# Decoder layer on one core: in the last group of heads VectorE turns the probabilities of tiles 0 and 1 and half of the values in 32x32 blocks

## The chip, the cores and the metric

The kernel runs on one core of a Trainium2 chip. The time is the device time of one execution in microseconds (us). The kernel before took 724.83 us, the median of 3 runs (724.61 to 726.72).

## The reference

A decoder layer on `x` of 8 sequences x 128 positions x 512 channels, in float32 (`_layernorm` has no weights):

```python
# 32 query heads, 8 key/value heads, head size 128; a group = 4 query heads and their key/value head
q, k, v = h @ w_q, h @ w_k, h @ w_v            # h = _layernorm(x)
scores  = einsum('bqhgd,bkhd->bhgqk', q, k) * 128 ** -0.5      # causal mask, softmax over keys
x = x + einsum('bhgqk,bkhd->bqhgd', probs, v).reshape(B, S, Hq * D) @ w_o
x = x + cross(ctx, ctx, _layernorm(x))         # softmax(ctx @ query^T), rows over query, then @ value
x = x + ffn(_layernorm(x))                     # silu(gate) * up, then down; weights unpacked from 4 bits
```

The output has the shape of `x`.

## The kernel before, in words

Every matmul of the attention is made in three passes: each operand is split into a rounded part (`_hi`) and the rest (`_lo`), and hi x hi, hi x lo and lo x hi are added in PSUM. ScalarE makes the hi parts by a copy; VectorE (out of PSUM) or GpSimd (out of SBUF) makes the lo parts by a subtraction.

There are 8 groups of heads (`LAST` is 7), and in each 8 tiles of 128 positions (tile b is sequence b). Groups 0 to 6 run as a loop with a deep pipeline of slots; the last group is written out by itself in `last_group`, one function for each engine, with 9 slots t = 0 to 8 and a short pipeline. Each engine takes its instructions strictly in the order in which its `last_group` issues them, and waits on semaphores. In a slot t:

- TensorE: `scores(t)`; the turning of the probabilities of tile t-1 through the array into PSUM bank `BK_T` (line 685, four 128x128 transposes); in slot 1 the turning of the second half of the values (`turn_values`, line 519); `fill` i, the projections of this group for the second half of the sequence range (12 matmuls each; 0 and 1 are keys and values, 2 to 5 queries) as `LAST_FILL` gives them; `values(t-1)` (probabilities x values, 3 matmuls); `out_heads(t-2)` (x `w_o`, 12 matmuls). From slot 3 on also `turn_queries(t-3)`, the first step of the cross attention of a tile. In slots 2 and 3 `out_heads` comes behind `values`, from slot 4 on (`EARLY`) ahead of it.
- VectorE: `mask(t)` (lines 1488 and 1492), `pt_lo` of tile t-1 (line 1543), `inverse(t)` (line 1498), `add_heads` (line 1424, which adds the output of `out_heads` to `xacc`), `heads_count` (lines 1288, 1289: mean and variance for the next layer norm), `heads_second(t-1)` (line 1503, `at_lo`).
- ScalarE: `pt_hi` of tile t-1 (line 996), `exponentials(t)` (line 919), the copies of the projections, `heads_first(t-1)` (line 951, `at_hi`), `second_norm(t-3)` (line 850, `xn`, the normalised tile that `turn_queries` turns), and in slots 0 and 1 the hi parts of the four `w_o` tiles (line 821).
- GpSimd: `normalise(t)` (line 1175), the lo parts of `w_o` (line 1160), and `inverse_deviation` (lines 1131 to 1136), which turns a variance into scale and shift for `xn`; in slot 2 for tile 0.

`out_heads(u)` of the last group always writes PSUM bank `BK_O`, so it waits until `add_heads(u-1)` has read it:

```python
pe.wait_ge(atlo_ready, step + u + 1 + PRIME)
pe.wait_ge(w_lo, g * UNITS + FIRST_UNITS + HG)
pe.wait_ge(o_added, step + u + PRIME - (g is not LAST))
```

In groups 0 to 6 the probabilities are turned by VectorE (`turn_probs`, line 1434: ten transposes of 32x32 blocks over four heads, the blocks above the diagonal being zero) from `probs` into the SBUF tile `pt`, and the values by sixteen such transposes (`turn_values`, line 1445) into `v_raw`; then GpSimd makes `pt_lo` and `v_lo`.

Of the kernel before, what the change touches and what calls it, by code (L numbers as in the profile page):

```python
# [7 lines left out]
ALU = mybir.AluOpType  # L8
# [14 lines left out]
PRIME = 2  # L23


def decoder_kernel(nc, x, ctx_in, ctx_turned, w_q, w_k, w_v, w_o,
# [26 lines left out]


    LAST_FILL = {0: [0, 1], 1: [2, 3], 2: [4], 3: [5]}
    LAST_TURN_V = 1
    LAST_SLOTS = NB + 1

    AT_NORM2, AT_SIM, AT_NORM3 = 3, 4, 6
# [21 lines left out]
    with ExitStack() as stack:  # L81
# [411 lines left out]
        def _(pe):  # L493
# [98 lines left out]
            def turn_queries(b):  # L592
                if 0 <= b < NB:
                    pe.wait_ge(ln_ready[1], b + 1)
                    if b >= 1:
                        pe.wait_ge(ln_hi[1], b)
                    else:
                        pe.wait_ge(vt_lo, NG * NH)
                    turn_tile(BK_XT, xn[:, b % 2, :]).then_inc(ln_turned[1], 1)

            def cross_output(b):
# [33 lines left out]
            def turn_values(g, n):  # L635

                pe.wait_ge(proj_out, g * NBLK + FIRST_BLOCKS + BLOCKS.index(("v", n)) + 1)
                pe.wait_ge(vt_lo, g * NH + (2 - n))
                turn_v(n)

            def fill(g, i):

                blocks = g * NBLK + FIRST_BLOCKS
                unit, n = BLOCKS[i]
                k = HBLK.index(unit)
                pe.wait_ge(w_lo, g * UNITS + (k + 1 if n == 1 else FIRST_UNITS + HG + k + 1))
                pe.wait_ge(proj_out, blocks + i - 1)
                project(unit, n, BK_PROJ[i % 2])
# [24 lines left out]
            def last_group():  # L673
                step = LAST * NB
                for t in range(LAST_SLOTS):
                    if t < NB:
                        scores(LAST, t)
                    if t >= 1:
                        u = t - 1
                        if u == 0:  # L680
                            pe.wait_ge(o_added, step + PRIME)
                        pe.wait_ge(prob_ready, step + u + 1)
                        pe.wait_ge(ptlo_ready, step + u + PRIME)
                        for j in range(HG):
                            mm = pe.transpose(psum[:, BK_T, j * P:(j + 1) * P], probs[:, u % 2, j, :], ident[:])
                        mm.then_inc(pt_done, 1)
                    if t == LAST_TURN_V:
                        turn_values(LAST, 1)
                    for i in LAST_FILL.get(t, ()):
                        fill(LAST, i)  # L690
                    cross_scores(t - AT_SIM)
                    if t >= EARLY:
                        out_heads(LAST, t - 2)
                    if t >= 1:
                        values(LAST, t - 1)
                    if 2 <= t < EARLY:
                        out_heads(LAST, t - 2)
                    turn_third(t - AT_NORM3)
                    turn_queries(t - AT_NORM2)
                    cross_output(t - AT_SIM)  # L700
# [117 lines left out]
        def _(act):  # L818
# [105 lines left out]
            def values_first(g, n):  # L924

                act.wait_ge(vt_done, 3 - n)
                act.wait_ge(pv_done, g * NB + (0 if n == 1 else BH) + PRIME)
                v_first(n)
# [60 lines left out]
            def last_group():  # L989
                step = LAST * NB  # L990
                for t in range(LAST_SLOTS):
                    if t >= 1:
                        u = t - 1
                        act.wait_ge(pt_done, u + 1 + PRIME)
                        act.wait_ge(pv_done, step + u + PRIME)
                        act.copy(pt_hi[:], psum[:, BK_T, :].rearrange("p (a b) -> p a b", a=HG)
                                 ).then_inc(pthi_ready, 1)
                    third_norm(t - AT_NORM3)
                    if t < NB:
                        exponentials(LAST, t)  # L1000
                    if t == LAST_TURN_V:
                        values_first(LAST, 1)
                    for i in LAST_FILL.get(t, ()):
                        fill_out(LAST, i)
                    if t >= EARLY:
                        cross_exp(t - AT_SIM)
                        second_norm(t - AT_NORM2)
                    if t >= 1:
                        heads_first(LAST, t - 1)
                    if t < EARLY:  # L1010
                        second_norm(t - AT_NORM2)
                    third(t - AT_NORM3)
                    queries_out(t - AT_NORM2)
                    for unit in SPLIT.get(t, ()):
                        if unit[0] == "o":
                            split_out(LAST, unit)
# [88 lines left out]
        def _(pool):  # L1105
# [66 lines left out]
            def normalise(g, t):  # L1172
# [3 lines left out]
                                   rowinv[:, t % 2, :].unsqueeze(2).to_broadcast([P, HG, P]),  # L1176
                                   ALU.mult).then_inc(prob_ready, 1)

            def group(g):
                n = 0  # L1180
                for t in range(SLOTS + 1):
                    if t in SPLIT_V:
                        half = slice(SPLIT_V[t] * BH, (SPLIT_V[t] + 1) * BH)
                        pool.wait_ge(vt_hi, g * NH + (3 - SPLIT_V[t]))
                        pool.tensor_tensor(v_lo[:, half, :], v_raw[:], v_hi[:, half, :].bitcast(F32),
                                           ALU.subtract).then_inc(vt_lo, 1)
                    if t < NB:
                        normalise(g, t)
                    if TURN <= t < NB + TURN:
                        pool.wait_ge(pthi_ready, g * NB + t - TURN + 1)  # L1190
                        pool.tensor_tensor(pt_lo[:], pt[:], pt_hi[:].bitcast(F32), ALU.subtract).then_inc(ptlo_ready, 1)  # L1191
                    for unit in SPLIT.get(t, ()):
                        n += 1
                        split_second(unit, g * UNITS + FIRST_UNITS + n)

            def last_group():
                n = 0
                for t in range(LAST_SLOTS):
                    if t < NB:
                        normalise(LAST, t)  # L1200
                    for unit in SPLIT.get(t, ()):
                        if unit[0] == "o":
                            n += 1
                            split_second(unit, LAST * UNITS + FIRST_UNITS + n)
                    cross(t)
# [69 lines left out]
        def _(dve):  # L1275
# [230 lines left out]
            def values_second(g, n):  # L1506

                dve.wait_ge(vt_hi, g * NH + (3 - n))
                v_second(n)
# [24 lines left out]
            def last_group():  # L1534
                step = LAST * NB
                for t in range(LAST_SLOTS):
                    if t < NB:
                        dve.wait_ge(pt_done, t - 1 + PRIME)
                        mask(LAST, t)
                    if t >= 1:  # L1540
                        u = t - 1
                        dve.wait_ge(pthi_ready, step + u + 1)
                        dve.tensor_tensor(pt_lo[:], psum[:, BK_T, :].rearrange("p (a b) -> p a b", a=HG),
                                          pt_hi[:].bitcast(F32), ALU.subtract).then_inc(ptlo_ready, 1)
                    cross_max(t - AT_SIM)
                    if 3 <= t < EARLY:
                        add_heads(LAST, t - 3)
                    if t < NB:
                        inverse(LAST, t)
                    cross_inverse(t - AT_SIM)  # L1550
                    if t > AT_SIM:
                        cross_add(t - AT_SIM - 1)
                        cross_count(t - AT_SIM - 1)
                    if t == EARLY - 1:
                        heads_count(LAST, t - 3)
                    if t >= EARLY:
                        add_heads(LAST, t - 2)
                        if t < NB:
                            heads_count(LAST, t - 2)
                    if t == LAST_TURN_V:  # L1560
                        values_second(LAST, 1)
                    if t >= 1:
                        heads_second(LAST, t - 1)
                    if t == EARLY:
                        scales()
                    if t == EARLY - 1:
                        add_heads(LAST, t - 2)
                        heads_count(LAST, t - 2)
                    if t == NB:
                        heads_count(LAST, t - 2)  # L1570
                    third_second(t - AT_NORM3)
# [152 lines left out]
```

## Time and profile before

| | us |
|---|---|
| median of 3 runs | 724.83 |
| the profiled execution | 724.8 |
| its span (first to last instruction) | 723.0 |
| TensorE busy | 705.2 (98%) |
| VectorE busy | 617.4 (85%) |
| ScalarE busy | 384.8 (53%) |
| GpSimd busy | 397.9 (55%) |
| the last group's slots 0 to 3 on TensorE | 501.5 to 532.3 |
| mean granted TensorE clock | 0.996 |

How to read it: the busy share of TensorE counts the time in which at least one matmul is in flight. In a timeline the difference between the starts of two matmuls is what one of them holds the engine; the duration shown is longer, since they overlap. A time in square brackets at the end of a timeline row is how long the engine sat idle before the instruction, and who released it.

### The profile page before, as it was taken

What the parts mean: (1) busy time and instruction counts of PE and PEld (TensorE: products, weight loads), DVE (VectorE), ACT (ScalarE), POOL (GpSimd) and SP (SyncE); (2) the same over time, 40 slices, a digit from 0 to 9 for tenths busy, and PEclk for the clock granted to TensorE, in tenths of its full rate; (3) what the DMA queues carried; (4) which work ended last, traced back from release to release, by engine and by line L of the source; (5) the groups of instructions that cost most, each with busy time, mean ns of one, the idle gap of its engine ahead of it and who ended that gap; (6) DMA issues with size and microseconds to landing.
All of it is one profiled execution on the core that took longest, in us unless ns stands there. A gap on an engine that the chain in (4) does not pass through costs nothing.

```text
span 723.0 us, 11410 instructions
## 1 busy us (share of the span) xinstructions
PE 705.2 (98%) x3450; PEld 586.2 (81%) x3450; DVE 617.4 (85%) x1387; ACT 384.8 (53%) x966; POOL 397.9 (55%) x376
## 2 busy tenths in 40 slices
PE   8999999999999999999999999999999889999995
PEld 8888888888888888888888888888877657888874
DVE  6589888988898898889888988988378888898897
ACT  4566535635562655365455636563556555655643
POOL 4375536545463655266445626561445535789886
PEclk9999999999999999999999999999999999999998
DMA  9523036105701550251046003402900002322103
GB/s 299 173 72 106 1 120 218 41 0 146 225 8 30 172 167 0 94 183 52 0 116 201 2 8 98 148 0 71 338 14 0 1 1 58 88 58 67 30 12 116
DMA packets 44902, 63.92 MB, mean 88 GB/s; under 512 B 4462, under 2 KB 23278, under 8 KB 44878
## 3 DMA queue, kind: packets, MB, share of 16 engines
q1 hardware_dynamic: 44878, 63.62, 28.3%
q8 instruction: 12, 0.20, 0.1%
q14 instruction: 12, 0.10, 0.1%
HBM read 52.67 MB, written 10.95 MB: 88 GB/s over the span
## 4 chain that ended last, share of the span: by engine, by line
PE 88%; DVE 5%; POOL 2%; ACT 2%; issue 2%; POOLq 0%; DVEq 0%; ACTq 0%
PE psum L500 21%; PE psum L499 21%; PE psum L501 21%; PE psum L630 8%; PE psum L716 5%; PE psum L717 5%; PE psum L739 2%; PE psum L738 2%; PE psum L526 1%; DVE stats L1288 1%; ACT probs L919 1%; PE psum L505 1%; POOL o_sum L1243 1%; DVE xprobs L1414 1%; DVE negmax L1492 0%
## 5 line engine op out<-in xcount | busy, mean ns | idle before, releaser
L1434 DVE STREAM_TRANSPOSE pt<-probs 32x128 f32<-32x128 f32 x560 | 168.9, 302 | 9.1 <-POOL pt_lo L1191 2.3
L1175 POOL TENSOR_TENSOR probs<-probs,rowinv 128x512 f32<-128x512 f32 x64 | 76.5, 1195 | 156.0 <-DVE rowinv L1498 156.0
L919 ACT ACTIVATE probs<-probs,negmax 128x128 f32<-128x128 f32 x256 | 99.9, 392 | 116.0 <-DVE negmax L1492 116.0
L499 PE MATMUL psum<-xt_hi,wq_hi 128*128 128x512 f32 x256 | 102.7, 401 | 0.0
L499 PE MATMUL psum<-wo_hi,at_hi 128*128 128x512 f32 x256 | 100.2, 392 | 0.5 <-DVE at_lo L1503 0.5
L501 PE MATMUL psum<-xt_hi,wq_lo 128*128 128x512 f32 x256 | 99.8, 390 | 0.0
L500 PE MATMUL psum<-xt_lo,wq_hi 128*128 128x512 f32 x256 | 99.8, 390 | 0.0
L501 PE MATMUL psum<-wo_hi,at_lo 128*128 128x512 f32 x256 | 99.6, 389 | 0.0
L500 PE MATMUL psum<-wo_lo,at_hi 128*128 128x512 f32 x256 | 99.6, 389 | 0.0
L1191 POOL TENSOR_TENSOR pt_lo<-pt,pt_hi 128x512 fp32r<-128x512 f32 x56 | 72.4, 1293 | 24.2 <-ACT pt_hi L982 24.1
L630 PEld LDWEIGHTS psum<-kt,qt 128*128 128x128 f32 x512 | 66.8, 191 | 6.5 <-issue 1.4
L716 PE MATMUL psum<-ft_hi,gw 128*128 128x512 f32 (+1 forms) x176 | 70.5, 400 | 1.2 <-DVE ft_lo L1297 0.9
L1445 DVE STREAM_TRANSPOSE v_raw<-vt 32x128 f32<-32x128 f32 x224 | 67.5, 301 | 3.5
L717 PE MATMUL psum<-ft_lo,gw 128*128 128x512 f32 (+1 forms) x176 | 69.0, 392 | 0.0
L630 PE MATMUL psum<-kt,qt 128*128 128x128 f32 x512 | 67.4, 274 | 0.3 <-ACT qt L833 0.3
L833 ACT ACTIVATE qt<-psum 128x512 f32<-128x512 f32 x64 | 37.7, 589 | 54.1 <-PE psum L501 54.0
L499 PEld LDWEIGHTS psum<-wo_hi,at_hi 128*128 128x128 f32 x256 | 48.1, 188 | 11.0 <-DVE at_lo L1503 1.2
L501 PEld LDWEIGHTS psum<-xt_hi,wq_lo 128*128 128x128 f32 x256 | 48.1, 188 | 10.1
L501 PEld LDWEIGHTS psum<-wo_hi,at_lo 128*128 128x128 f32 x256 | 48.0, 188 | 10.0
L1424 DVE TENSOR_TENSOR xacc<-psum,xacc 128x512 f32<-128x512 f32 x64 | 44.1, 688 | 14.2 <-PE psum L501 12.5
L500 PEld LDWEIGHTS psum<-wo_lo,at_hi 128*128 128x128 f32 x256 | 48.1, 188 | 9.8
L951 ACT CAST at_hi<-psum 128x512 fp32r<-128x512 f32 x64 | 37.1, 579 | 35.6 <-PE psum L501 34.3
(158 smaller groups left out, 1576.2 us busy)
## 6 DMA issues: line engine op xcount, KB each, us to landing
wq_raw<-in_L_attn_w_q SPq DMA_DIRECT2D x8, 1024.0 KB, 5.6
wo_raw<-in_L_attn_w_o SPq DMA_DIRECT2D x8, 1024.0 KB, 7.8
u_zn<-zeros_gu SPq DMA_DIRECT2D x16, 344.0 KB, 6.3
unpacked_w<-u_q SPq DMA_DIRECT2D x8, 688.0 KB, 7.8
gw<-unpacked_w SPq DMA_DIRECT2D x20, 256.0 KB, 3.5
unpacked_w<-u_q SPq DMA_DIRECT2D x6, 512.0 KB, 6.7
u_q<-in_L_ffn_gate_qweight SPq DMA_DIRECT2D x8, 344.0 KB, 5.7
u_q<-in_L_ffn_up_qweight SPq DMA_DIRECT2D x8, 344.0 KB, 4.1
```

Of the source, the lines that this page charges most:

```text
L499: pe.matmul(dst, a_hi, b_hi, start=start, stop=False)
L500: pe.matmul(dst, a_hi, b_lo, start=False, stop=False)
L501: return pe.matmul(dst, a_lo, b_hi, start=False, stop=stop)
L630: mm = pe.matmul(psum[:, BK_S, j * P:(j + 1) * P], qt[:, j, t * P:(t + 1) * P], kt[:, t * P:(t + 1) * P], start=True, stop=True)
L716: pe.matmul(dst, gw[:, r, m, c, 0:w], ft_hi[:, c, cols], start=True, stop=False)
L717: return pe.matmul(dst, gw[:, r, m, c, 0:w], ft_lo[:, c, cols], start=False, stop=True)
L919: e = act.activation(probs[:, t % 2, j, :], probs[:, t % 2, j, :], ACT.Exp, bias=negmax[:, t % 2, j:j + 1], accum_out=rowsum[:, t % 2, j:j ...
L1175: pool.tensor_tensor(probs[:, t % 2], probs[:, t % 2], rowinv[:, t % 2, :].unsqueeze(2).to_broadcast([P, HG, P]), ALU.mult).then_inc(prob_ ...
L1191: pool.tensor_tensor(pt_lo[:], pt[:], pt_hi[:].bitcast(F32), ALU.subtract).then_inc(ptlo_ready, 1)
L1424: dve.tensor_tensor(xacc[:, u, :], psum[:, out_bank(g, u), :], xacc[:, u, :], ALU.add).then_inc(o_added, 1)
L1434: turned = dve.transpose(pt[keys, :, queries], probs[queries, t % 2, :, keys])
L1445: turned = dve.transpose(v_raw[keys, :, heads], vt[heads, n, :].rearrange("p (a b) -> p a b", a=BH)[:, :, keys])
```

## The change

In the last group, tiles 0 and 1 (`LAST_BLOCKS` = 2) are now turned by VectorE with `turn_probs` into `pt`, in slots 0 and 1; their `pt_hi` is copied by ScalarE from `pt`, and their `pt_lo` made by GpSimd (`probs_second`). The second half of the values is turned by VectorE in slots 1 (6 blocks) and 2 (10 blocks); its hi part is copied by ScalarE in slot 3, its lo part made by GpSimd in slot 3, ahead of `normalise(3)`. Tiles 2 to 7 are turned by TensorE as before. On TensorE, the turning of tile 2 in slot 3 moves behind `fill` 5, and `out_heads` stands ahead of `values` in slots 2 and 3 too. `turn_queries(0)` waits for one `vt_lo` less.

```diff
--- before.py
+++ after.py
@@ -53,7 +53,9 @@
 
 
     LAST_FILL = {0: [0, 1], 1: [2, 3], 2: [4], 3: [5]}
-    LAST_TURN_V = 1
+    LAST_BLOCKS = 2
+    LAST_TURN_V = {1: (0, 6), 2: (6, 16)}
+    LAST_SPLIT_V = 3
     LAST_SLOTS = NB + 1
 
     AT_NORM2, AT_SIM, AT_NORM3 = 3, 4, 6
@@ -595,7 +597,7 @@
                     if b >= 1:
                         pe.wait_ge(ln_hi[1], b)
                     else:
-                        pe.wait_ge(vt_lo, NG * NH)
+                        pe.wait_ge(vt_lo, NG * NH - 1)
                     turn_tile(BK_XT, xn[:, b % 2, :]).then_inc(ln_turned[1], 1)
 
             def cross_output(b):
@@ -675,25 +677,27 @@
                 for t in range(LAST_SLOTS):
                     if t < NB:
                         scores(LAST, t)
-                    if t >= 1:
+                    if t == LAST_BLOCKS + 1:
+                        for i in LAST_FILL[t]:
+                            fill(LAST, i)
+                    if t > LAST_BLOCKS:
                         u = t - 1
-                        if u == 0:
+                        if u == LAST_BLOCKS:
                             pe.wait_ge(o_added, step + PRIME)
                         pe.wait_ge(prob_ready, step + u + 1)
                         pe.wait_ge(ptlo_ready, step + u + PRIME)
                         for j in range(HG):
                             mm = pe.transpose(psum[:, BK_T, j * P:(j + 1) * P], probs[:, u % 2, j, :], ident[:])
                         mm.then_inc(pt_done, 1)
-                    if t == LAST_TURN_V:
-                        turn_values(LAST, 1)
-                    for i in LAST_FILL.get(t, ()):
-                        fill(LAST, i)
+                    if t != LAST_BLOCKS + 1:
+                        for i in LAST_FILL.get(t, ()):
+                            fill(LAST, i)
                     cross_scores(t - AT_SIM)
-                    if t >= EARLY:
+                    if t >= EARLY or 2 <= t <= LAST_BLOCKS + 1:
                         out_heads(LAST, t - 2)
                     if t >= 1:
                         values(LAST, t - 1)
-                    if 2 <= t < EARLY:
+                    if LAST_BLOCKS + 1 < t < EARLY:
                         out_heads(LAST, t - 2)
                     turn_third(t - AT_NORM3)
                     turn_queries(t - AT_NORM2)
@@ -991,15 +995,18 @@
                 for t in range(LAST_SLOTS):
                     if t >= 1:
                         u = t - 1
-                        act.wait_ge(pt_done, u + 1 + PRIME)
+                        if u < LAST_BLOCKS:
+                            act.wait_ge(pt_turned, step + u + 1)
+                        else:
+                            act.wait_ge(pt_done, u - LAST_BLOCKS + 1 + PRIME)
                         act.wait_ge(pv_done, step + u + PRIME)
-                        act.copy(pt_hi[:], psum[:, BK_T, :].rearrange("p (a b) -> p a b", a=HG)
-                                 ).then_inc(pthi_ready, 1)
+                        act.copy(pt_hi[:], pt[:] if u < LAST_BLOCKS else
+                                 psum[:, BK_T, :].rearrange("p (a b) -> p a b", a=HG)).then_inc(pthi_ready, 1)
+                    if t == LAST_SPLIT_V:
+                        values_rounded(LAST, 1)
                     third_norm(t - AT_NORM3)
                     if t < NB:
                         exponentials(LAST, t)
-                    if t == LAST_TURN_V:
-                        values_first(LAST, 1)
                     for i in LAST_FILL.get(t, ()):
                         fill_out(LAST, i)
                     if t >= EARLY:
@@ -1176,19 +1183,27 @@
                                    rowinv[:, t % 2, :].unsqueeze(2).to_broadcast([P, HG, P]),
                                    ALU.mult).then_inc(prob_ready, 1)
 
+            def values_second(g, n):
+
+                half = slice(n * BH, (n + 1) * BH)
+                pool.wait_ge(vt_hi, g * NH + (3 - n))
+                pool.tensor_tensor(v_lo[:, half, :], v_raw[:], v_hi[:, half, :].bitcast(F32),
+                                   ALU.subtract).then_inc(vt_lo, 1)
+
+            def probs_second(g, u):
+
+                pool.wait_ge(pthi_ready, g * NB + u + 1)
+                pool.tensor_tensor(pt_lo[:], pt[:], pt_hi[:].bitcast(F32), ALU.subtract).then_inc(ptlo_ready, 1)
+
             def group(g):
                 n = 0
                 for t in range(SLOTS + 1):
                     if t in SPLIT_V:
-                        half = slice(SPLIT_V[t] * BH, (SPLIT_V[t] + 1) * BH)
-                        pool.wait_ge(vt_hi, g * NH + (3 - SPLIT_V[t]))
-                        pool.tensor_tensor(v_lo[:, half, :], v_raw[:], v_hi[:, half, :].bitcast(F32),
-                                           ALU.subtract).then_inc(vt_lo, 1)
+                        values_second(g, SPLIT_V[t])
                     if t < NB:
                         normalise(g, t)
                     if TURN <= t < NB + TURN:
-                        pool.wait_ge(pthi_ready, g * NB + t - TURN + 1)
-                        pool.tensor_tensor(pt_lo[:], pt[:], pt_hi[:].bitcast(F32), ALU.subtract).then_inc(ptlo_ready, 1)
+                        probs_second(g, t - TURN)
                     for unit in SPLIT.get(t, ()):
                         n += 1
                         split_second(unit, g * UNITS + FIRST_UNITS + n)
@@ -1196,6 +1211,10 @@
             def last_group():
                 n = 0
                 for t in range(LAST_SLOTS):
+                    if 1 <= t <= LAST_BLOCKS:
+                        probs_second(LAST, t - 1)
+                    if t == LAST_SPLIT_V:
+                        values_second(LAST, 1)
                     if t < NB:
                         normalise(LAST, t)
                     for unit in SPLIT.get(t, ()):
@@ -1535,9 +1554,14 @@
                 step = LAST * NB
                 for t in range(LAST_SLOTS):
                     if t < NB:
-                        dve.wait_ge(pt_done, t - 1 + PRIME)
+                        if 2 <= t < LAST_BLOCKS + 2:
+                            dve.wait_ge(pt_turned, step + t - 1)
+                        elif t >= LAST_BLOCKS + 2:
+                            dve.wait_ge(pt_done, t - 1 - LAST_BLOCKS + PRIME)
                         mask(LAST, t)
-                    if t >= 1:
+                    if t in LAST_TURN_V:
+                        turn_values(LAST, 1, *LAST_TURN_V[t])
+                    if t > LAST_BLOCKS:
                         u = t - 1
                         dve.wait_ge(pthi_ready, step + u + 1)
                         dve.tensor_tensor(pt_lo[:], psum[:, BK_T, :].rearrange("p (a b) -> p a b", a=HG),
@@ -1557,8 +1581,8 @@
                         add_heads(LAST, t - 2)
                         if t < NB:
                             heads_count(LAST, t - 2)
-                    if t == LAST_TURN_V:
-                        values_second(LAST, 1)
+                    if t < LAST_BLOCKS:
+                        turn_probs(LAST, t)
                     if t >= 1:
                         heads_second(LAST, t - 1)
                     if t == EARLY:
```

## Rows read from the trace of the kernel before

**Rows 1.** The page of the profile, busy time and the chain that ended last.

```profile
PE 705.2 (98%) x3450; PEld 586.2 (81%) x3450; DVE 617.4 (85%) x1387; ACT 384.8 (53%) x966; POOL 397.9 (55%) x376
...
PE 88%; DVE 5%; POOL 2%; ACT 2%; issue 2%; POOLq 0%; DVEq 0%; ACTq 0%
```

**Rows 2.** Timeline, TensorE, slots 1 to 4 (start us, duration us, engine, line, tiles).

```profile
508.69 0.60 PE L685 MATMUL psum<-ident,probs 128*128 128x128 f32 x4
509.13 0.60 PE L519 MATMUL psum<-ident,vt 128*128 128x128 f32 x4
509.49 0.48 PE L499 MATMUL psum<-xt_hi,wq_hi 128*128 128x512 f32 x1
...
515.02 0.39 PE L499 MATMUL psum<-pt_hi,v_hi 128*128 128x512 f32 x1
...
520.48 0.39 PE L499 MATMUL psum<-wo_hi,at_hi 128*128 128x512 f32 x1
...
523.21 1.05 PE L630 MATMUL psum<-kt,qt 128*128 128x128 f32 x8
524.09 0.60 PE L685 MATMUL psum<-ident,probs 128*128 128x128 f32 x4
524.45 0.48 PE L499 MATMUL psum<-xt_hi,wq_hi 128*128 128x512 f32 x1
...
527.30 0.39 PE L499 MATMUL psum<-pt_hi,v_hi 128*128 128x512 f32 x1
...
527.98 0.39 PE L499 MATMUL psum<-wo_hi,at_hi 128*128 128x512 f32 x1
...
531.76 0.66 PE L505 MATMUL psum<-ident,xn 128*128 128x128 f32 x4 [0.89 <-ACT xn L850]
```

**Rows 3.** Timeline, VectorE, the same slots.

```profile
505.75 0.18 DVE L1498 RECIPROCAL rowinv<-rowsum 128x4 f32<-128x4 f32 x1 [1.72 <-ACT probs L919]
...
509.69 0.69 DVE L1492 TENSOR_REDUCE negmax<-probs 128x4 f32<-128x512 f32 x1
...
525.69 0.68 DVE L1543 TENSOR_TENSOR pt_lo<-psum,pt_hi 128x512 fp32r<-128x512 f32 x1
526.29 0.68 DVE L1424 TENSOR_TENSOR xacc<-psum,xacc 128x512 f32<-128x512 f32 x1
527.50 0.18 DVE L1498 RECIPROCAL rowinv<-rowsum 128x4 f32<-128x4 f32 x1 [0.53 <-ACT probs L919]
```

**Rows 4.** Timeline, ScalarE, group 6 (first row) and the same slots.

```profile
466.12 0.62 ACT L982 CAST pt_hi<-pt 128x512 fp32r<-128x512 f32 x1 [0.45 <-DVE pt L1434]
...
504.06 0.40 ACT L919 ACTIVATE probs<-probs,negmax 128x128 f32<-128x128 f32 x1 [2.42 <-DVE negmax L1492]
...
524.73 0.59 ACT L996 CAST pt_hi<-psum 128x512 fp32r<-128x512 f32 x1 [3.46 <-PE psum L685]
...
530.89 0.81 ACT L850 ACTIVATE xn<-xacc,shift,rstd 128x512 f32<-128x512 f32 x1 [2.12 <-POOL shift L1136]
```

**Rows 5.** Timeline, GpSimd, the same slots.

```profile
506.01 1.04 POOL L1175 TENSOR_TENSOR probs<-probs,rowinv 128x512 f32<-128x512 f32 x1 [3.00 <-DVE rowinv L1498]
...
517.09 2.55 POOL L1160 TENSOR_TENSOR wo_lo<-wo_raw,wo_hi 128x512 fp32r<-128x512 f32 x2 [3.69 <-ACT wo_hi L821]
```

**Rows 6.** Timeline, VectorE, group 6, where it turns probabilities.

```profile
462.95 3.13 DVE L1434 STREAM_TRANSPOSE pt<-probs 32x128 f32<-32x128 f32 x10
```

**Rows 7.** Timeline, TensorE, its two longest idle times behind the start.

```profile
706.47 0.50 PE L738 MATMUL psum<-int_hi,dw 128*128 128x512 f32 x1 [1.09 <-DVE o_sum L1642]
...
713.94 1.86 PE L812 MATMUL psum<-ident,o 128*128 128x128 f16 x16 [1.26 <-POOL o L1262]
```

**Rows 8.** Windows near the end: PE, PEld, DVE, ACT, POOL busy; granted clock; DMA.

```profile
713.00:714.00 1.00, 0.06 (x1) 0.09 (x2) 1.00 (x3) 0.40 (x1) 1.00 (x2) 0.99 0.00 0
714.00:715.00 1.00, 1.00 (x11) 1.00 (x12) 1.00 (x3) 0.00 (x0) 1.00 (x2) 0.50 0.00 0
...
717.00:718.00 1.00, 0.91 (x12) 0.73 (x10) 0.98 (x2) 0.28 (x1) 0.78 (x1) 0.81 1.03 385
```

## Prediction, made before the changed kernel was run

> **What bounds the kernel now.** I read the page first: TensorE is busy for 98% of the span and carries 88% of the chain that ended last [rows 1]. So a change elsewhere costs or gives only what it does to TensorE's order of work. Then I read the timelines of the last group, since the diff touches nothing else, TensorE first. From 508.69 to 530.87 one matmul follows the other; the only idle time is the 0.89 us before `turn_queries(0)` at 531.76, which waits for `xn` [rows 2]. The timelines of the three other engines show what stands in front of that `xn` [rows 3 to 5]. From slot 4 on the diff changes no order, so the question is only how much later or earlier `turn_queries(0)` starts; what follows is built on it and on itself, and I take it to move as a block.
>
> **What TensorE is spared.** The turning of tile 0 held it 0.44 us (509.13 less 508.69), that of the values 0.36 (509.49 less 509.13), that of tile 1 as much as tile 2, 0.36 (524.45 less 524.09) [rows 2]. Sum 1.16 us. Moving the turning of tile 2 behind `fill` 5 and `out_heads` ahead of `values` removes no work.
>
> **What VectorE gains in work.** Ten blocks of probabilities take 3.13 us [rows 6], twice 6.26; the values' sixteen blocks at the same 0.313 each 5.0. It is spared three subtractions of 0.68 [rows 3], 2.0. Net 9.2 us more in slots 0 to 2, where it was mostly idle. I follow it in order of time, with the handovers of the rows.
>
> Slots 0 and 1. `inverse(0)` at 505.75, `normalise(0)` on GpSimd 506.01 to 507.05 [rows 3, 5]. Turn tile 0: 507.1 to 510.24. `mask(1)` can't start before, so its second instruction stands at 511.0 where it stood at 509.69 [rows 3]. Six blocks of the values: to 513.5. `exponentials(1)` starts 0.7 us after that second instruction, and the inverse 1.69 after the exponentials' start (505.75 less 504.06 [rows 3, 4]), 513.4: both are ready at 513.5. `normalise(1)` to 514.8; turn tile 1: 514.85 to 518.0. Then `at_lo(0)`, to 518.7. TensorE meanwhile has no transposes: `fill` 2 and 3 (5.53 us, 515.02 less 509.49) from 508.7 to 514.2, `values(0)` 0.68 to 514.9, `scores(2)` 0.88, `fill` 4 2.85, to 518.6 [rows 2]. GpSimd makes `pt_lo(0)` from 511.7 to 513.0, in time.
>
> Slot 2. `out_heads(0)` was at 520.48 behind `values(1)` [rows 2]; now it stands directly behind `fill` 4 and wants `at_lo(0)` (518.7) and the last `w_o` lo part. That one starts with ScalarE's copies, which follow `at_hi(0)`, 0.8 us earlier than before: GpSimd 516.3 where it was 517.09, plus 2.55, 518.85 [rows 5]. TensorE waits about 0.3 us; `out_heads(0)` 518.9 to 521.7 (2.73, 523.21 less 520.48, and 0.1 for the first matmul after a wait), `values(1)` to 522.3, `scores(3)` to 523.2, `fill` 5 to 526.05. On VectorE `mask(2)`, then ten blocks of values, 519.9 to 523.1, `inverse(2)`, `at_lo(1)` to 523.9, `mask(3)` to 525.2. `prob_ready(2)` is there at 524.4, ahead of the turning. All this is covered by `fill` 5.
>
> Slot 3. The turning of tile 2 starts at 526.05 and ends at 526.4, where it ended at 524.45 [rows 2]. Now cover is missing. `pt_hi(2)` starts 0.25 later, T = 526.65 (it was 524.73, 0.28 after the turning [rows 4]). VectorE sits at `pt_lo(2)` until T + 0.62, and queued behind it is `add_heads(0)`, T + 1.22 to T + 1.9 (0.60 from start to start, 0.68 long [rows 3]). `out_heads(1)` uses the same bank and waits for that add. Before, `fill` 5 and `values(2)` stood between the turning and `out_heads(1)`: 527.98 less 524.45, 3.53 us of cover, and the add was over by 526.97 [rows 2, 3]. Now nothing stands between them. TensorE idles from 526.4 to T + 1.95 = 528.6: **2.2 us**. Then `out_heads(1)` 2.84 to 531.4, `values(2)` to 532.1.
>
> `turn_queries(0)`. Two chains lead to `xn(0)`. One: `exponentials(3)` on ScalarE is queued behind `pt_hi(2)` and the new copy of `v_hi` (0.52 each from start to start), so it starts at T + 1.05 = 527.7, `inverse(3)` at 529.4, where it was 527.50; from there to `xn(0)` it was 3.39 us (530.89 less 527.50 [rows 3, 4]), so 532.8. Two: ScalarE's `at_hi(2)` is queued ahead of `xn(0)` and wants `values(2)`: 532.1 + 0.2 + 0.5 = 532.8. Both end at once. TensorE turns at 532.8 + 0.87 = 533.65 (531.76 less 530.89) and has idled 1.5 us instead of 0.89. So **+1.9 us** at this point. Check by the account: 0.3 + 2.2 + 1.5 idle less 0.89, less 1.16 spared, is 1.95. GpSimd's new `v_lo` (1.3) stands ahead of `normalise(3)`; it ends at 535.0 and TensorE wants it at 535.05 behind `scores(4)`: free, by a hair.
>
> GpSimd's subtraction out of SBUF, 1.3 us where VectorE took 0.68, and ScalarE's copy out of `pt`, 0.62 where it took 0.59 out of PSUM [rows 4], are in these times. No transfer is touched.
>
> **The clock.** An idle time of 1.26 us near the end, before line 812, was followed by the clock's fall from 2.4 to 1.2 GHz (0.99 granted in 713 to 714, 0.50 in 714 to 715); it was back at full speed within 717 to 718, whose mean of 0.81 puts the return at 717.4. The idle of 1.09 us before 706.47 was not followed by a fall [rows 7, 8]. The change makes an idle time of 2.2 us with transposes ahead of it, and one of 1.5. Longer than the one that led to a fall: I take it that the clock falls once here. A stretch of 3.4 us at half speed, full of matmuls of `out_heads(1)` and `values(2)`, costs at most 1.7 us; part of it may lie in the idle time, so 1.6. The second chain to `xn(0)` passes it on whole.
>
> The Trainium skill (TensorE: Matmul & The Clock Gate, section Why this matters for your kernels) warns only of idle gaps longer than this change makes; by that rule the clock stays and the time is that of the first rival. The trace has a fall after 1.26 us, which speaks against leaning on it.
>
> The Trainium skill (VectorE: DVE Perf Modes, section Rules for kernel authors) says that a 128x128 transpose belongs on TensorE where PSUM will do as its destination. The rows agree on the price, 0.36 us of TensorE against 3.13 of VectorE for a tile of four heads [rows 2, 6]; had VectorE no idle time the change would cost some 9 us. It has it in slots 0 to 2.
>
> **The sum.** The profiled execution took 724.8 us (span 723.0), which is the median too: 724.8 + 1.9 + 1.6 = **728.3 us**.
>
> **Rivals.**
> - *The clock stays at 2.4 GHz.* For it: idle times of 0.89 and 1.09 us left it alone, and dense matmuls stand around these. Against: 1.26 led to a fall. Then 724.8 + 1.9 = 726.7, which is not slower by what can be told. If the fall comes in some executions alone, the median is one of the two.
> - *The waits are covered after all* (`add_heads(0)` is over in time, `xn(0)` no later in relation to the work). Then only the spared 1.16 us is left, 723.6. The code speaks against it: bank, order and wait are fixed. Even with the 0.89 us gone too it would be 722.7, so hardly faster by 0.3%.
> - *Turning the tiles by VectorE takes longer and more is late*: if the blocks of tile 1 and its `at_lo(0)` came 1 us later (GpSimd's order, blocks slowed by it), `out_heads(0)` and all behind it would move by the same; with the fall 729.3.
> - *The chain's length is over-told*: both chains and the 2.2 us shrink by some tenths each, and some later wait absorbs a part. Then 725.5 to 726.5.
>
> **Chances.** A measurement here can tell about 0.3%, 2.2 us: faster is below 722.65, slower above 727.0. Fall of the clock 0.50 (nearly all slower); clock stays 0.32 (a quarter of it above 727.0); more is late 0.06; chain over-told 0.09; covered 0.03. So slower 0.64, same 0.34, faster 0.02. Range: from 725.9, which leaves out 0.1 at the bottom, to 729.2, which takes in a late `out_heads(0)` beside the fall.
>
> **What would show it.** Right: TensorE idle about 2.2 us before the first matmul of `out_heads(1)` (line 499, `wo_hi`), released by VectorE's add to `xacc`; idle about 1.5 us before the first turning of `xn`; ten blocks of 3.13 us twice; the granted clock at 0.50 for some us from about 529. Wrong: the granted clock at 1.00 there (then 726.7); `out_heads(1)` without idle; a shift at `scores(5)` other than at `turn_queries(0)`; or idle before `out_heads(0)` of much over 0.3 us.

## The result and the profile after

The changed kernel took 728.34 us, the median of 6 runs (727.94 to 728.76), against 724.83 us of before, the median of 6 (724.59 to 726.72). The ratio is 1.004 (95% interval 1.0028 to 1.0051): slower by 3.5 us. The forecast was 728.3.

The page after, busy times and shares of the chain, which answer to [rows 1]:

```profile
PE 706.3 (97%) x3438; PEld 586.2 (81%) x3438; DVE 626.1 (86%) x1420; ACT 384.4 (53%) x966; POOL 401.1 (55%) x379
...
PE 87%; DVE 6%; POOL 3%; issue 2%; ACT 2%; POOLq 0%; DVEq 0%; ACTq 0%
```

TensorE has 12 matmuls fewer, VectorE 8.7 us more work, and the span went from 723.0 to 726.6. The busy shares tell nothing of where 3.6 us went. The timeline of TensorE in the last group does (it answers to [rows 2]; start, duration, engine, line, tiles, idle time before and who released it). The first row is `scores(0)`, where the last group starts:

```profile
501.55 1.05 PE L632 MATMUL psum<-kt,qt 128*128 128x128 f32 x8
...
518.96 0.47 PE L501 MATMUL psum<-wo_hi,at_hi 128*128 128x512 f32 x1 [0.24 <-DVE at_lo L1522]
...
526.11 0.60 PE L690 MATMUL psum<-ident,probs 128*128 128x128 f32 x4
...
528.79 0.47 PE L501 MATMUL psum<-wo_hi,at_hi 128*128 128x512 f32 x1 [2.09 <-DVE xacc L1443]
...
532.94 0.63 PE L501 MATMUL psum<-pt_hi,v_hi 128*128 128x512 f32 x1
...
535.46 0.66 PE L507 MATMUL psum<-ident,xn 128*128 128x128 f32 x4 [1.39 <-ACT xn L854]
```

Three idle times stand in it. The second, 2.09 us before `out_heads(1)`, is new and is ended by line 1443, the add into `xacc`. `out_heads(1)` then takes 4.15 us (532.94 less 528.79) where twelve matmuls took 2.73 [rows 2].

VectorE in slot 3 (it answers to [rows 3]):

```profile
527.36 0.69 DVE L1567 TENSOR_TENSOR pt_lo<-psum,pt_hi 128x512 fp32r<-128x512 f32 x1 [2.06 <-ACT pt_hi L1003]
527.97 0.68 DVE L1443 TENSOR_TENSOR xacc<-psum,xacc 128x512 f32<-128x512 f32 x1
529.42 0.18 DVE L1517 RECIPROCAL rowinv<-rowsum 128x4 f32<-128x4 f32 x1 [0.78 <-ACT probs L923]
```

It sat idle for 2.06 us at `pt_lo(2)` with `add_heads(0)` queued behind it, although `out_heads(0)` had been issued in full by 521.8 (518.96 plus 2.84), 6.2 us before the add started. ScalarE's rows answer to [rows 4]:

```profile
526.74 0.58 ACT L1003 CAST pt_hi<-psum 128x512 fp32r<-128x512 f32 x1 [3.48 <-PE psum L690]
527.22 0.62 ACT L938 CAST v_hi<-v_raw 128x512 fp32r<-128x512 f32 x1
...
534.11 0.58 ACT L955 CAST at_hi<-psum 128x512 fp32r<-128x512 f32 x1 [4.23 <-PE psum L503]
534.59 0.82 ACT L854 ACTIVATE xn<-xacc,shift,rstd 128x512 f32<-128x512 f32 x1
```

`xn` stands behind `at_hi(2)`, which waits for `values(2)`: the second chain of the prediction. And the granted clock (window; PE, PEld, DVE, ACT, POOL busy; granted share of the clock; DMA share, GB/s):

```profile
529.00:530.00 1.00, 1.00 (x5) 0.81 (x5) 0.58 (x2) 0.87 (x4) 0.00 (x0) 1.00 0.00 0
530.00:531.00 1.00, 1.00 (x4) 0.78 (x3) 0.36 (x2) 0.00 (x0) 0.38 (x2) 0.55 0.00 0
...
533.00:534.00 1.00, 1.00 (x4) 0.54 (x2) 0.00 (x0) 0.00 (x0) 1.00 (x2) 0.74 0.00 0
```

The clock fell from 2.4 to 1.2 GHz at about 530.1 and came back at about 533.5.

Executions start a few tenths of a microsecond apart, so I measure from the start of `scores(0)` to the start of the first turning of `xn`, `turn_queries(0)`. Before it is 531.76 less 501.46 (the row of `scores(0)` below), 30.30 us:

```profile
501.46 1.05 PE L630 MATMUL psum<-kt,qt 128*128 128x128 f32 x8
```

After it is 535.46 less 501.55, 33.91: +3.61 us, which is all of the span's 3.6. In the experiments this distance carries the main readings: where a kernel was profiled more than once it agrees to 0.05 us (33.86 to 33.91 in three profiles, 33.13 and 33.18 in two), while the runs of before alone spread over 2 us. It ends at `turn_queries(0)`, so what happens behind that point isn't in it; where it matters I give the distance to a later instruction too.

### The profile page after: what moved, and what is told of

The parts are those of the page before. It is cut to its first block, busy times and chain, and to the rows that moved or that the text cites. A ratio compares the mean times of both kernels' runs of the same rounds, so it can differ in the third digit from the quotient of the medians.

```text
span 726.6 us, 11420 instructions
## 1 busy us (share of the span) xinstructions
PE 706.3 (97%) x3438; PEld 586.2 (81%) x3438; DVE 626.1 (86%) x1420; ACT 384.4 (53%) x966; POOL 401.1 (55%) x379
## 4 chain that ended last, share of the span: by engine, by line
PE 87%; DVE 6%; POOL 3%; issue 2%; ACT 2%; POOLq 0%; DVEq 0%; ACTq 0%
PE psum L501 21%; PE psum L503 21%; PE psum L502 21%; PE psum L632 8%; PE psum L720 5%; PE psum L721 5%; PE psum L743 2%; PE psum L742 2%; PE psum L528 1%; DVE stats L1307 1%; PE psum L507 1%; ACT probs L923 1%; POOL o_sum L1262 1%; DVE xprobs L1433 1%; DVE xacc L1485 0%
## 5 line engine op out<-in xcount | busy, mean ns | idle before, releaser
L1453 DVE STREAM_TRANSPOSE pt<-probs 32x128 f32<-32x128 f32 x580 | 175.0, 302 | 11.7 <-POOL probs L1182 2.3
L1196 POOL TENSOR_TENSOR pt_lo<-pt,pt_hi 128x512 fp32r<-128x512 f32 x58 | 75.0, 1293 | 24.2 <-ACT pt_hi L986 24.1
L1464 DVE STREAM_TRANSPOSE v_raw<-vt 32x128 f32<-32x128 f32 x240 | 72.3, 301 | 3.7
L501 PEld LDWEIGHTS psum<-xt_hi,wq_hi 128*128 128x128 f32 x256 | 48.2, 188 | 8.8
```

What stands on the lines that cost most here:

```text
L501: pe.matmul(dst, a_hi, b_hi, start=start, stop=False)
L1453: turned = dve.transpose(pt[keys, :, queries], probs[queries, t % 2, :, keys])
L1464: turned = dve.transpose(v_raw[keys, :, heads], vt[heads, n, :].rearrange("p (a b) -> p a b", a=BH)[:, :, keys])
```

## The experiments

**e1_busy: is part of the loss the clock's?** The changed kernel with work in the idle time:

```diff
+                    if t == LAST_BLOCKS + 1:
+                        for _ in range(10):
+                            pe.matmul(psum[:, BK_VT, 0:P], ident[:], ident[:], start=True, stop=True)
                     if t >= EARLY or 2 <= t <= LAST_BLOCKS + 1:
                         out_heads(LAST, t - 2)
```

> The changed kernel, and in slot 3, between the turning of tile 2 and out_heads(1), ten small matmuls (128x128, identity x identity) into a PSUM bank that nothing reads then, so that TensorE is not idle while it waits for add_heads(0); the order and every wait stay. If 1.7 us of the loss is the clock's fall that the idle time brings (theory): granted clock 1.00 from 520 to 540, out_heads(1) 2.85 us long where it is 4.15, turn_queries(0) at 533.7 where it is 535.5, time 728.3 - 1.7 = 726.6. If the clock has no part in the time (rival): turn_queries(0) at 535.5 and 728.3.

726.71 us (725.96 to 728.52, 7 runs), ratio to before 1.0032 (1.0018 to 1.0045). TensorE's timeline and the windows:

```profile
526.31 0.60 PE L690 MATMUL psum<-ident,probs 128*128 128x128 f32 x4
526.75 2.40 PE L698 MATMUL psum<-ident 128*128 128x128 f32 x20
529.00 0.47 PE L501 MATMUL psum<-wo_hi,at_hi 128*128 128x512 f32 x1
...
534.06 0.66 PE L507 MATMUL psum<-ident,xn 128*128 128x128 f32 x4 [1.39 <-ACT xn L857]
```

```profile
528.00:532.00 4.00, 4.00 (x24) 3.48 (x23) 1.80 (x5) 2.08 (x10) 1.02 (x4) 1.00 0.00 0
532.00:534.00 2.00, 0.67 (x3) 0.21 (x2) 0.68 (x2) 1.29 (x2) 1.79 (x4) 1.00 0.00 0
```

The ten matmuls stand in the profile as twenty instructions and fill the gap; `out_heads(1)` starts as long after the turning of tile 2 as before (2.69 us, 2.68 in the changed kernel). With useless matmuls in the gap the clock stays at 1.00, `out_heads(1)` takes 2.83 us (to 531.83), and the distance is 32.28 (534.06 less 501.78): +1.98. So the loss of 3.6 is 2.0 of waiting and 1.6 of clock. The median too is 1.6 us below that of the changed kernel, but the two intervals of the ratio overlap, so the split rests on the profile. In that profile a kernel that does more work is faster.

**e2_add: only `add_heads(0)` ahead of `pt_lo(2)`.**

```diff
+                    if t == EARLY - 1:
+                        add_heads(LAST, t - 3)
                     if t > LAST_BLOCKS:
                         u = t - 1
                         dve.wait_ge(pthi_ready, step + u + 1)
...
-                    if 3 <= t < EARLY:
-                        add_heads(LAST, t - 3)
```

> The changed kernel with add_heads(0) ahead of pt_lo(2) on VectorE in slot 3. Theory: the 2.1 us of idle time before out_heads(1) goes (out_heads(1) at 526.5), but heads_count(0) still stands behind inverse(3), which waits for exponentials(3) behind pt_hi(2), so xn(0) starts at 532.8 and turn_queries(0) at 533.7; TensorE idles 3.7 us before it instead. Time 726.7 if the clock stays, up to 728.4 if it falls after that idle time. Rival (only the wait for the bank matters): 728.3 - 2.1 - 1.7 = 724.5.

728.62 us (727.47 to 730.99, 4 runs), ratio 1.0064 (1.0042 to 1.0086).

```profile
525.89 0.60 PE L690 MATMUL psum<-ident,probs 128*128 128x128 f32 x4
...
533.46 0.66 PE L507 MATMUL psum<-ident,xn 128*128 128x128 f32 x4 [3.54 <-ACT xn L854]
...
535.01 1.06 PE L690 MATMUL psum<-ident,probs 128*128 128x128 f32 x4
```

`out_heads(1)` has no idle time any more, and nothing is won: TensorE idles 3.54 us before `xn` instead. The distance is 32.10 (533.46 less 501.36), +1.80, as without a fall of the clock. The fall came later: the granted clock was 0.58 from 534 to 538, and the turning of a tile at 535.01 lasted 1.06 us instead of 0.60. That fall lies behind the end of the distance; measured to `turn_queries(1)`, this kernel has 39.87 (541.23 less 501.36) where before had 36.48 (537.94 less 501.46), +3.39, nearly all of the changed kernel's loss. The rival that only the wait for the bank matters (724.5) is out. The median lies 0.2 above the upper end expected.

**e3_count: `heads_count(0)` too.**

```diff
                     if t == EARLY - 1:
                         add_heads(LAST, t - 3)
+                        heads_count(LAST, t - 3)
```

(and taken away behind `inverse(3)`).

> As the run before, and heads_count(0) too stands ahead of pt_lo(2). Theory: now the only thing ahead of xn(0) is at_hi(2) on ScalarE, after values(2) at 529.9: xn(0) 530.6, turn_queries(0) 531.5, TensorE idle 1.6 us before it, clock at 1.00, time 724.5. Rival (VectorE's blocks in slots 0 to 2 are what costs, not the order in slot 3): little of the 3.6 us comes back, over 727.

724.51 us (723.53 to 726.31, 10 runs), ratio 1.0001 (0.9991 to 1.001). All of the loss is gone, with the same blocks on VectorE.

```profile
530.88 0.66 PE L507 MATMUL psum<-ident,xn 128*128 128x128 f32 x4 [1.39 <-ACT xn L854]
```

The distance is 29.92 (530.88 less 500.96), 0.38 under before. With TensorE's order as changed, what costs is where two short steps stand in VectorE's queue, not the 9 us of blocks.

**e5_turn: the turning of tile 2 ahead of `fill` 5 again.**

```diff
-                    if t == LAST_BLOCKS + 1:
-                        for i in LAST_FILL[t]:
-                            fill(LAST, i)
                     if t > LAST_BLOCKS:
...
-                    if t != LAST_BLOCKS + 1:
-                        for i in LAST_FILL.get(t, ()):
-                            fill(LAST, i)
+                    for i in LAST_FILL.get(t, ()):
+                        fill(LAST, i)
```

> The changed kernel with the turning of tile 2 ahead of fill 5, where it stood before. Theory: TensorE waits for prob_ready(2) at 524.5 (1.2 to 1.3 us idle, the price of VectorE's ten blocks of values ahead of inverse(2)), but fill 5 covers pt_hi(2), pt_lo(2) and add_heads(0): no idle before out_heads(1), turn_queries(0) at 532.8, idle 1.6 us before it; time 725.7 if the clock stays, up to 1.7 more if it falls. Rival (blocks cost, order doesn't): 728.

725.9 us (725.4 to 726.12, 10 runs), ratio 1.0015 (1.0005 to 1.0025).

```profile
524.65 0.63 PE L687 MATMUL psum<-ident,probs 128*128 128x128 f32 x4 [1.14 <-issue]
...
532.81 0.66 PE L507 MATMUL psum<-ident,xn 128*128 128x128 f32 x4 [1.39 <-ACT xn L850]
```

The cover is back, the 2.09 us before `out_heads(1)` are gone, and TensorE waits 1.14 us for `prob_ready(2)` instead (the row names no releaser; GpSimd's `normalise(2)` started at 523.51 and took 1.04, to 524.55). The distance is 31.24 (532.81 less 501.57), +0.94, and the clock stayed at 1.00. So there was a reason to move the turning, and the move costs more than it saves as long as VectorE's order stays. `out_heads` still stands ahead of `values` here, so the 2.09 us come from the move of the turning, and not from that exchange.

**e6_order: TensorE's order alone, on the kernel before.** No blocks; line 685 turns all tiles.

```diff
+                    if t == 3:
+                        for i in LAST_FILL[t]:
+                            fill(LAST, i)
                     if t >= 1:
                         u = t - 1
...
-                    if t >= EARLY:
+                    if t >= EARLY or 2 <= t <= 3:
                         out_heads(LAST, t - 2)
                     if t >= 1:
                         values(LAST, t - 1)
-                    if 2 <= t < EARLY:
-                        out_heads(LAST, t - 2)
```

> The kernel before, with TensorE's order of the changed one alone: in slot 3 fill 5 ahead of the turning of tile 2, in slots 2 and 3 out_heads ahead of values. No block is turned by VectorE. Theory (the order makes the loss): turning of tile 2 ends at 527.3, add_heads(0) over at 529.4, idle 2.1 us before out_heads(1), turn_queries(0) at 534.6 with the clock at 1.00 and 536.2 with a fall: time 727.5, or 729.1 with the fall. Rival (the blocks make it): within 0.5 us of before, 724.8 to 725.3.

727.69 us (727.21 to 728.85, 4 runs), ratio 1.0039 (1.0024 to 1.0055).

```profile
529.45 0.47 PE L499 MATMUL psum<-wo_hi,at_hi 128*128 128x512 f32 x1 [2.09 <-DVE xacc L1426]
...
534.52 0.66 PE L505 MATMUL psum<-ident,xn 128*128 128x128 f32 x4 [1.39 <-ACT xn L852]
```

```profile
529.00:532.00 3.00, 2.55 (x11) 2.15 (x12) 1.24 (x4) 1.01 (x5) 1.10 (x4) 1.00 0.00 0
```

(The lines left out at the second mark take `fill` 5 away from its old place.) The same two idle times, 2.09 and 1.39, without any block, and the distance is 33.18 (534.52 less 501.34), +2.88. The clock stayed at 1.00 in this profile. With e1_busy the account closes: the order costs 2.88, the blocks give back 0.9 (1.16 of transposes less 0.24 of idle time before `out_heads(0)`), the clock takes 1.6: 3.6.

**e8_look, e9_look, e10_look: does the clock always fall?** The changed kernel twice more and e6_order once more, unaltered.

> The changed kernel unaltered, one more profiled execution. If the clock falls behind this idle time in every execution: granted clock 0.50 for 3.4 us from about 530 again, out_heads(1) about 4.15 us long. If it depends on the execution (as the order's profile suggests, where 2.09 us of the same idle time left the clock at 1.00): in some looks 1.00 and out_heads(1) 2.84 us long, turn_queries(0) 1.7 us earlier.

> As e8_look, another execution of the same kernel, for the same question: the fall there or not, and the time with it, 728.3 with the fall and 726.7 without.

> The kernel e6_order once more (TensorE's order alone), one profiled execution: its idle time before out_heads(1) is 2.1 us again; the clock stays at 1.00 if something in that kernel keeps it there, and falls in this one or not if it depends on the execution.

One run each: 728.43, 727.78 and 727.34 us. The changed kernel in e8_look:

```profile
528.00:529.00 1.00, 0.12 (x1) 0.16 (x1) 0.73 (x2) 1.00 (x7) 0.00 (x0) 0.91 0.00 0
...
530.00:531.00 1.00, 1.00 (x4) 0.81 (x3) 0.45 (x2) 0.00 (x0) 0.34 (x2) 0.50 0.00 0
```

and in e9_look:

```profile
530.00:531.00 1.00, 1.00 (x4) 0.81 (x3) 0.12 (x1) 0.00 (x0) 0.62 (x3) 0.50 0.00 0
```

The fall is there in three profiles of three of the changed kernel (distances 33.91, 33.87 and 33.86), and absent in two of two of e6_order (33.18 and 33.13), whose idle time of 2.09 us is as long and ends 0.9 us later, counted from `scores(0)` (28.11 against 27.24). So the length of the idle time doesn't settle it.

Is it chance? Two things in the traces say that chance has a part. First, the fall doesn't stand at a fixed place in the changed kernel: worked out from the granted shares of each microsecond it began at 530.10, 528.82 and 528.96, which is 1.3 us behind the start of `out_heads(1)`, with it, and 0.4 us behind it; each time it lasted 3.4 us and cost the same. Second, one and the same idle time near the end, the 1.26 to 1.30 us before the first turning of `o` (line 812 of before, [rows 7]), stands in all twelve profiles of this case. In five of them (before, after, e4_early, e7_before_early, e10_look) the clock fell within 0.4 us of its end; in the seven others it stayed at 1.00 through the sixteen matmuls. This is e1_busy's row, 1.05 us long where before's is 1.86:

```profile
716.15 1.05 PE L819 MATMUL psum<-ident,o 128*128 128x128 f16 x16 [1.27 <-POOL o L1284]
```

There the fall depends on the execution: e6_order and e10_look, one kernel, are on different sides, and so are the changed kernel's first profile and its two repeats. For the gap of 2.09 us, three of three against two of two can't be told from chance either: with three falls dealt out over five profiles at random, one deal in ten is this one. The times lean the other way: all eight executions of the changed kernel took 727.78 to 728.76, none near the 726.7 of a kept clock. Whether something in e6_order keeps the clock up stays open.

**e4_early: a version that uses the change.** As e3_count, and on ScalarE in slot 3 `exponentials(3)` first and `xn(0)` ahead of `at_hi(2)`:

```diff
                 for t in range(LAST_SLOTS):
+                    if t == EARLY - 1:
+                        exponentials(LAST, t)
                     if t >= 1:
...
-                    if t < NB:
+                    if t < NB and t != EARLY - 1:
                         exponentials(LAST, t)
...
                     if t >= EARLY:
                         cross_exp(t - AT_SIM)
-                        second_norm(t - AT_NORM2)
+                    second_norm(t - AT_NORM2)
```

(and taken away behind `heads_first`).

> As e3_count, and on ScalarE in slot 3 exponentials(3) ahead of pt_hi(2), which waits for TensorE, and second_norm(0) ahead of heads_first(2). Theory: xn(0) no longer waits for values(2), only for the statistics at 526.8 + 2.3 on GpSimd and the queue: xn(0) at 529.3, turn_queries(0) at 530.2 where it was 531.8 before the change; the 1.16 us spared and most of the 0.9 us idle are both gained: 724.8 - 1.6 = 723.2. Rival (the spared transposes are given back in VectorE's later slots, or GpSimd's v_lo ahead of normalise(3) becomes the wait): turn_queries(0) early, but the turning of tile 3 at 532 or later and 724 or more.

724.25 us (724.1 to 725.46, 11 runs); before in the same hour 725.1; ratio 0.9988 (0.9979 to 0.9997). By the times it is 0.9 us faster than before, half of what was expected, with an interval that just clears 1.

```profile
529.99 0.65 PE L507 MATMUL psum<-ident,xn 128*128 128x128 f32 x4
...
536.97 0.66 PE L507 MATMUL psum<-ident,xn 128*128 128x128 f32 x4 [0.62 <-ACT xn L854]
```

`turn_queries(0)` has no idle time and comes at 28.58 (529.99 less 501.41), 1.72 us earlier than before, as expected. The next tile's comes with 0.62 us of idle time, at 35.56 where before had 36.48 (537.94 less 501.46): 0.92 is left. VectorE shows why:

```profile
530.64 0.69 DVE L1522 TENSOR_TENSOR at_lo<-psum,at_hi 128x512 fp32r<-128x512 f32 x1 [2.51 <-ACT at_hi L955]
531.25 0.68 DVE L1443 TENSOR_TENSOR xacc<-psum,xacc 128x512 f32<-128x512 f32 x1
531.96 0.69 DVE L1307 BATCH_NORM_STATS2 stats<-xacc 128x6 f32<-128x512 f32 x1
532.69 0.18 DVE L1308 BATCH_NORM_AGGREGATE meanvar<-stats 128x2 f32<-128x6 f32 x1
532.79 0.67 DVE L1507 TENSOR_TENSOR probs<-psum,causal 128x512 f32<-128x512 f32 x1
```

`at_lo(2)` and the statistics of tile 1 stand ahead of `mask(4)`, which so starts 1.41 us behind the end of `scores(4)` (531.38) instead of 0.27; the exponentials and, queued behind them, `xn(1)` follow late. I had not followed slot 4 for this kernel. At the first matmul of the feed-forward part (`gw`, start 580.52) 0.70 is left: 79.11 from `scores(0)`, before 79.81 (581.27 less 501.46). The profiled execution also had a fall of the clock from 591.0 to 594.5, behind an idle time of 0.94 us that left the clock alone before (0.93) and in e3_count (0.94).

**e7_before_early: the earlier statistics without blocks.** The kernel before with `heads_count(0)` ahead of `inverse(3)`.

```diff
                     if 3 <= t < EARLY:
                         add_heads(LAST, t - 3)
+                        heads_count(LAST, t - 3)
                     if t < NB:
                         inverse(LAST, t)
...
-                    if t == EARLY - 1:
-                        heads_count(LAST, t - 3)
```

> The kernel before with heads_count(0) ahead of inverse(3) on VectorE in slot 3, which e3_count's move amounts to here; nothing else. Theory: xn(0) 0.5 us earlier, turn_queries(0) at 531.2, time 724.3. It tells what of e4_early's gain is the blocks' (the 1.16 us of TensorE) and what the earlier statistics': 0.9 us at most could come from these, so a version without blocks can't be under 723.9, and e4_early at 723.2 would be 0.7 under that.

725.46 us (723.8 to 725.93, 11 runs), ratio 1.0 (0.9991 to 1.0009).

```profile
530.79 0.66 PE L505 MATMUL psum<-ident,xn 128*128 128x128 f32 x4 [0.34 <-ACT xn L850]
```

In the profile `turn_queries(0)` is at 29.74 (530.79 less 501.05), 0.56 earlier, with 0.34 us of idle time left; the median doesn't show it, and half a microsecond is inside its interval. By the times this run is inconclusive. It was to tell what of e4_early's gain is the blocks', and it doesn't settle that: at the first `gw` matmul its profile is 0.56 ahead of before (79.25 less 79.81) and e4_early's 0.70, 0.14 apart, while the medians of the same hour are 1.2 us apart. A version with e4_early's order on ScalarE and no blocks was not run.

## Why the prediction was right, point by point

- *What TensorE is spared*, 1.16 us, and the price of the blocks, 3.13 us for ten: the blocks took 3.14 to 3.15 in each of the three tens. Right.
- *0.3 us before `out_heads(0)`*: 0.24 in the bracket, ended by `at_lo`.
- *2.2 us before `out_heads(1)`*: 2.09 in the bracket, ended by the add. That this is TensorE's order and not the blocks is shown by e6_order, where it is 2.09 without any; that VectorE's queue carries it is shown by e2_add.
- *Two chains to `xn(0)`, ending at once*: the prediction's sharpest claim. In e1_busy, with the clock up, GpSimd has written the shift by 532.98 and `xn(0)` starts behind `at_hi(2)` at 533.19, so the chains end 0.2 apart. e2_add takes the bank's wait away and comes to +1.80 where e1_busy has +1.98, a gain of 0.2; e3_count shortens the first chain too and comes to -0.38, a gain of 2.4. Shortening the first chain alone was not run on the changed kernel.
- *1.5 us before `turn_queries(0)`*: 1.39 in the bracket. It is 1.39 in each of the changed kernel, e1_busy, e3_count, e5_turn and e6_order, with blocks or without: in all of them `out_heads(1)` stands ahead of `values(2)`, and nothing on TensorE covers `at_hi(2)` and `xn(0)` behind it. That exchange alone was not run, so its price is read from these rows and not tested.
- *The sum without the clock*: forecast +1.9, measured +1.98. The brackets give less, 0.24 + 2.09 + 1.39 - 0.89 - 1.16 = 1.67, since a bracket starts at the end of the last matmul's record, which is longer than what that matmul holds the engine. From holds the three waits are 0.41 (518.96 less 518.32 and 0.23), 2.32 (528.79 less 526.11 and 0.36) and, in e1_busy, 1.55 (534.06 less 531.83 and 0.68), and that of before is 1.05 (531.76 less 530.48 and 0.23). The prediction took its own three from holds and before's 0.89 from the bracket. That 0.16 too much and the 0.1 too little in each of its first two waits nearly cancel.
- *The block from slot 4 on moves as a whole*: +3.61 at `turn_queries(0)`, +3.58 at `turn_queries(1)` (541.61 less 501.55, less 36.48), +3.6 at the end. It held for the change, but not for e4_early, where the shift shrank from 1.72 to 0.92 within one slot.
- *The clock*: forecast 1.6, measured 1.6 by e1_busy (33.91 less 32.28). The size was worked out soundly; that the fall came at all was luck in part, and the prediction itself gave it 0.50. It rested on one fall after 1.26 us, and the same idle time brings that fall in five of the twelve profiles only; e6_order has 2.09 us and no fall. With the clock up the result would have been the first rival's 726.7, which is e1_busy's time.
- *GpSimd's `v_lo` ahead of `normalise(3)`*, free by a hair: `normalise(3)` ended at 535.0 and the clock's fall had moved its reader to 536.8, so the changed kernel doesn't test it. e1_busy does: with the clock up it ended at 535.21 and its reader, the turning of tile 3, started at 535.44 without idle time.

The advice of the Trainium skill (VectorE: DVE Perf Modes, section Rules for kernel authors) to turn 128x128 tiles on TensorE, which the prediction named, doesn't decide here. The blocks take VectorE 3.14 us a tile where TensorE took 0.36 to 0.44, but they fall into VectorE's idle time: e3_count has all the blocks and the time of before.

## What to carry to other kernels

When an engine's work is moved to another, ask first which idle time covered the steps right behind the moved ones. Here 1.2 us were saved on the bound engine and 2.9 lost because a transpose was put directly ahead of a matmul that waits, through another engine's queue, for what the transpose sets off. In an in-order queue an instruction that has long been ready (`add_heads(0)`: its input was complete by 522.0, it started at 527.97) should not stand behind one that waits; and where two chains end together, a repair of one is worth little until both are made (0.2 us in e2_add, 2.4 in e3_count).

## What the runs showed of the hardware

A wait in the middle of a dense stretch can cost nearly twice its length: 2.09 us of idle time were followed by 3.4 us at 1.2 GHz in three profiles of three, worth 1.6 us, and with ten matmuls without purpose in the gap the clock stayed at 2.4 GHz and the 1.6 us came back (one profile). As long an idle time, 0.9 us later in the program, was followed by no fall in two of two, and at one of 1.26 to 1.30 us near the end the clock fell in five profiles of twelve. So a single profile with a fall, or without one, says little about the next execution.

The Trainium skill (TensorE: Matmul & The Clock Gate, section Why this matters for your kernels) warns only of idle gaps longer than these. Here gaps of 2.09 and 1.26 us were followed by falls, so the measurement goes against taking gaps as short as these for safe.
